# Moving one PSUM bank from the QKV projection to the attention scores in a fused attention and linear kernel

## The chip, the cores and the metric

The kernel runs on all 8 cores of one Trainium2 chip. Each core takes one of 8 batch entries and the cores exchange nothing. Time is device microseconds (us) of the slowest core, lower is better.

## What is computed

For each batch entry x of 2048 x 2048 (tokens x features): layer norm, a causal attention with 16 heads of width 128, layer norm and residual, then a linear layer with binarized weights, layer norm and residual. The attention has no exponentials: it takes the fourth power of the scores.

```python
def _L0_attn_ref(x, w_qkv, w_out, ln_scale, ln_bias):
    proj = x @ w_qkv
    q, k, v = jnp.split(proj, 3, axis=-1)          # 16 heads of 128 each
    ...
    q = layernorm(apply_rope(q, cos, sin), ln_scale, ln_bias)
    k = layernorm(apply_rope(k, cos, sin), ln_scale, ln_bias)
    a = jnp.einsum('bhnd,bhmd->bhnm', q, k) ** 4
    a = jnp.tril(a)
    out = jnp.einsum('bhnm,bhmd->bhnd', a / jnp.sum(a, -1, keepdims=True), v)
    return out.reshape(b, n, e) @ w_out
x = x + _layernorm(_L0_attn_ref(_layernorm(x), ...))
x = x + _layernorm(_layernorm(x) @ binarized(weight).T + bias)
```

## The kernel before

A helper records the operations of each engine in program order and derives semaphore waits from the tiles that each operation reads and writes. An engine works its own list strictly in order, so the order in which units are recorded is the order on each engine.

Three stages follow each other behind fences. The first normalizes x and runs the heads, the second projects with w_out, the third is the linear layer. Only the first uses the tiles of this change.

The first stage keeps the normalized, transposed x in SBUF (LNXT) and goes over heads h = 0 to 16. Step h does the QKV projection of head h and, interleaved with it, the attention of head h - 1.

- Projection: `u_m(m)` for m = 0 to 15 (blocks of 128 tokens). TensorE accumulates 16 matmuls (line 342) into one PSUM bank PQ, 384 columns wide (q, k and v). VectorE then reads it three times: two multiplies for the rotation (lines 348 and 352) and a copy of v into VPAD (line 357). Two additions with sums (line 363) follow on VectorE and two squarings with sums on ScalarE (line 372). PQ has two banks, used in turn. After the 16 blocks come `u_smalls` (mean and variance), 16 `u_norm` (line 407) and `u_final` (transposes by DMA, then scaling on ScalarE, lines 433 and 437).
- Attention: for each of four query blocks i and key blocks j up to 4i + 3, `u_s` makes one score matmul into a PSUM bank PS (line 457), and ScalarE squares it (line 464, reading PS) and squares it again (line 467). On the diagonal VectorE multiplies 128 columns by a triangle (line 471). `u_pv` does the value matmuls (line 482) of unit j - 4. At the end of a query block the last four are done and VectorE and ScalarE make the quotient (lines 492 to 508). PS has two banks by j % 2. The value sums have four banks, PV. With PQ and PS that is all eight PSUM banks.

The order: 34 projection units and 45 attention units are merged. With SHIFT = 3 the blocks m = 0 to 3 are issued with no attention unit between them; behind each later block come one or two (19 by the end of block 15), and the other 26 run beside `u_smalls` and the norms, where TensorE has no projection. At the end of a head's step VectorE has the signs and sums of one piece of the linear layer's weight (`swt_unit`, lines 566 to 579).

Of the kernel before, what the change touches and what calls it, by code (L numbers as in the profile page):

```python
# [8 lines left out]
F32 = mybir.dt.float32  # L9
# [172 lines left out]
def build_nc():  # L182
    nc = bass.Bass("TRN2", target_bir_lowering=False)
# [17 lines left out]
    P = Prog()  # L201
    with contextlib.ExitStack() as top:
# [48 lines left out]
        with contextlib.ExitStack() as sA:  # L251
            TA = sA.enter_context
# [16 lines left out]
            T1 = [TA(nc.sbuf_tensor(f"T1{i}", [128, 256], F32)) for i in range(2)]  # L269
# [11 lines left out]
            VPAD = [TA(nc.sbuf_tensor(f"VPAD{i}", [128, MC * 129], BF16))  # L281
                    for i in range(2)]
            S2B = [TA(nc.sbuf_tensor(f"S2B{i}", [128, 512], BF16)) for i in range(4)]
            S4B = [TA(nc.sbuf_tensor(f"S4B{i}", [128, 512], BF16)) for i in range(6)]
            PQ = [TA(nc.psum_tensor(f"PQ{i}", [128, 512], F32)) for i in range(2)]
            PS = [TA(nc.psum_tensor(f"PS{i}", [128, 512], F32)) for i in range(2)]
            PV = [TA(nc.psum_tensor(f"PV{i}", [128, 512], F32)) for i in range(4)]

            for i in range(2):
# [43 lines left out]
            def qkv_units(h):  # L333
                par = h % 2
                units = []
                wkeys = [f"wh{par}/{t_i}" for t_i in range(3)]

                def u_m(m):
                    b = m % 2
                    pqk = f"pq{b}"  # L340
                    for kc in range(KC):
                        P.op("t", lambda t, m=m, kc=kc, par=par, b=b: t.matmul(  # L342
                            PQ[b][:, 0:384],
                            LNXT[:, kc * N + m * 128: kc * N + m * 128 + 128],
                            WH[par][:, kc * 384:(kc + 1) * 384],
                            start=(kc == 0), stop=(kc == KC - 1)),
                            reads=[f"lnxT/{kc}/{m}"] + wkeys, writes=[pqk])
                    P.op("v", lambda v, b=b, m=m: v.tensor_tensor(  # L348
                        T1[b][:], PQ[b][:, 0:256],
                        AP(CT, m * 128, [[MC * 128, 128], [0, 2], [1, 128]]),  # L350
                        AOT.mult), reads=[pqk, "CT"], writes=[f"t1{b}"])
                    P.op("v", lambda v, b=b, m=m: v.tensor_tensor(  # L352
                        T2[b][:],
                        AP(PQ[b], 64, [[512, 128], [128, 2], [-64, 2], [1, 64]]),
                        AP(ST, m * 128, [[MC * 128, 128], [0, 2], [1, 128]]),
                        AOT.mult), reads=[pqk, "ST"], writes=[f"t2{b}"])
                    P.op("v", lambda v, b=b, m=m, par=par: v.tensor_copy(  # L357
                        VPAD[par][:, m * 129: m * 129 + 128], PQ[b][:, 256:384]),
                        reads=[pqk], writes=[f"vpad{par}/{m}"])
                    for t_i in range(2):  # L360
                        col = 2 * m + t_i
                        P.op("v", lambda v, b=b, m=m, t_i=t_i, col=col:
                             v.scalar_tensor_tensor(  # L363
                                 QR[:, m * 256 + t_i * 128:
                                    m * 256 + t_i * 128 + 128],
                                 T1[b][:, t_i * 128:(t_i + 1) * 128], cp(C_ZERO),
                                 T2[b][:, t_i * 128:(t_i + 1) * 128],
                                 AOT.add, AOT.add,
                                 accum_out=SUMS[:, col:col + 1]),
                             reads=[f"t1{b}", f"t2{b}", "CP0"],  # L370
                             writes=[f"qr/{m}/{t_i}", f"sums/{col}"])
                        P.op("s", lambda s, m=m, t_i=t_i, col=col: s.activation(  # L372
                            P4S[col % 4][:],
                            QR[:, m * 256 + t_i * 128: m * 256 + t_i * 128 + 128],
                            ACTF.Square, accum_out=SS[:, col:col + 1]),
                            reads=[f"qr/{m}/{t_i}"],
                            writes=[f"p4s{col % 4}", f"ssq/{col}"])
                for m in range(MC):
                    units.append(lambda m=m: u_m(m))

                def u_smalls():
                    sumkeys = [f"sums/{c_}" for c_ in range(32)]
                    sskeys = [f"ssq/{c_}" for c_ in range(32)]
                    P.op("v", lambda v: v.tensor_scalar(
                        MEANS[:], SUMS[:], cp(C_I128), None, AOT.mult,
                        AOT.bypass), reads=sumkeys + ["CP1"], writes=["means"])
                    P.op("v", lambda v: v.tensor_scalar(
                        SMA[:], SS[:], cp(C_I128), None, AOT.mult, AOT.bypass),
                        reads=sskeys, writes=["sma"])
                    P.op("v", lambda v: v.tensor_tensor(  # L390
                        SMB[:], MEANS[:], MEANS[:], AOT.mult),
                        reads=["means"], writes=["smb"])
                    P.op("v", lambda v: v.tensor_tensor(
                        SMA[:], SMA[:], SMB[:], AOT.subtract),
                        reads=["sma", "smb"], writes=["sma"])
                    P.op("s", lambda s: s.activation(
                        SMB[:], SMA[:], ACTF.Sqrt, bias=cp(C_EPS)),
                        reads=["sma"], writes=["smb"])
                    P.op("v", lambda v: v.reciprocal(RQ[:], SMB[:]),  # L399
                         reads=["smb"], writes=["rq"])  # L400
                units.append(u_smalls)

                def u_norm(m):
                    for t_i in range(2):
                        col = 2 * m + t_i
                        P.op("v", lambda v, m=m, t_i=t_i, col=col:
                             v.tensor_scalar(  # L407
                                 QN[:, t_i * N + m * 128:
                                    t_i * N + m * 128 + 128],
                                 QR[:, m * 256 + t_i * 128:  # L410
                                    m * 256 + t_i * 128 + 128],
                                 MEANS[:, col:col + 1], RQ[:, col:col + 1],
                                 AOT.subtract, AOT.mult),
                             reads=[f"qr/{m}/{t_i}", "means", "rq"],
                             writes=[f"qn/{m}/{t_i}"])
                for m in range(MC):
                    units.append(lambda m=m: u_norm(m))

                def u_final():
                    qnkeys = [f"qn/{m}/{t}" for m in range(MC)  # L420
                              for t in range(2)]
                    for t_i, dst, nm in ((0, QFM, "qfm"), (1, KFM, "kfm")):
                        P.dma("y", lambda y, t_i=t_i, dst=dst, par=par:
                              y.dma_start_transpose(
                                  AP(dst[par], 0,
                                     [[N, 128], [128, 16], [1, 128]]),
                                  QN[:, t_i * N:(t_i + 1) * N]),
                              reads=qnkeys,
                              writes=[f"{nm}{par}/{m}" for m in range(MC)],
                              slot=f"qnT{t_i}")  # L430
                    qk = [f"qfm{par}/{m}" for m in range(MC)]
                    kk = [f"kfm{par}/{m}" for m in range(MC)]
                    P.op("s", lambda s, par=par: s.activation(
                        QFM[par][:], QFM[par][:], ACTF.Identity, bias=BET[:],
                        scale=GAM[:]),
                        reads=qk + ["GAM", "BET"], writes=[f"qfmF{par}"] + qk)
                    P.op("s", lambda s, par=par: s.activation(
                        KFM[par][:], KFM[par][:], ACTF.Identity, bias=BET[:],
                        scale=GAM[:]),
                        reads=kk + ["GAM", "BET"], writes=[f"kfmF{par}"] + kk)  # L440
                units.append(u_final)
                return units

            def attn_units(hh):
# [4 lines left out]
                def u_s(i, j):  # L449
# [1 line left out]
                    s0 = 128 * max(0, r)  # L451
                    nj = 512 - s0
                    jb = j % 6
                    pb_ = j % 2
                    psk = f"ps{pb_}"
                    P.op("t", lambda t, i=i, j=j, s0=s0, nj=nj, pb_=pb_,
                         par=par: t.matmul(  # L457
# [458 lines left out]
```

How the kernel before makes its waits and increments, by code:

```python
    def emit_one(self, e, eng, sems, slot_sems):  # L135
        waited = {}
        drained = -1
        for i, op in enumerate(self.streams[e]):
            for sk, val in op.dma_waits:
                hs = slot_sems[sk]
                if waited.get(id(hs), -1) < val:
                    eng.wait_ge(hs, val)
                    waited[id(hs)] = val
            for dep, dval in op.deps:
                if dep.slot is not None:
                    hs = slot_sems[dep.slot]
                    val = dval
                else:
                    hs = sems[dep.eng]
                    val = dep.cum
                if waited.get(id(hs), -1) < val:
                    eng.wait_ge(hs, val)
                    waited[id(hs)] = val
            if op.drain_upto > drained:
                eng.drain()
                drained = i - 1
            if op.fn is None:
                if op.inc and e in sems:
                    eng.nop().then_inc(sems[e], 1)
                continue
            inst = op.fn(eng)
            if op.slot is not None:
                inst.then_inc(slot_sems[op.slot], 16)
            elif op.inc:
                inst.then_inc(sems[e], 1)
```

## Time and profile before

| | |
|---|---|
| median of 2 runs | 2498.98 us (2496.86 to 2501.1) |
| the profiled execution's own time | 2510.83 us |
| its span, slowest core (core 5) | 2509.3 us |
| spans of the 8 cores | 2462.0 to 2509.3 us |
| PE busy | 1629.7 us (65%), 8960 matmuls |
| ACT busy | 1200.3 us (48%) |
| DVE busy | 1014.7 us (40%) |

PE is TensorE's matmul side and PEld its weight loads, DVE is VectorE, ACT is ScalarE, POOL is GpSimd. Busy shares are means over the three stages. A timeline row gives an engine's work merged over like instructions; the last duration of a run of matmuls includes the pipeline's depth, so a block of 16 reads 2.76 us although blocks can follow each other every 2.60. PEclk is the granted TensorE clock, 1.00 for 2.4 GHz and 0.50 for 1.2 GHz. The brackets name the idle time before an instruction and what ended it.

### The profile page before, as it was taken

The page shows a single profiled execution, that of the slowest core. Times are in us where ns is not written, and L with a number is a line of the kernel's source. Part 1 is how long each engine was busy: PE and PEld are TensorE (multiplying, and loading weights), DVE is VectorE, ACT ScalarE, POOL GpSimd, SP SyncE. Part 2 cuts the span into 40 slices and gives each one's busy share as a digit, 9 for nine tenths or more (in the row PEclk, how much of TensorE's full clock was granted, in tenths as well). Part 3 has the DMA queues.
Part 4 walks back from the last instruction along what each step waited for, and adds up shares of the span by engine and source line. Part 5 has one row for each costly group of instructions (what it writes and reads, how often), then busy time and mean ns, then how long its engine had stood idle before and what let it go on. Part 6 is the DMA issues. An engine that isn't in the chain of part 4 may idle for free.

```text
span 2509.3 us, 32780 instructions; the slowest of 8 cores (2462.0 to 2509.3 us)
## 1 busy us (share of the span) xinstructions
PE 1629.7 (65%) x8960; PEld 860.8 (34%) x8960; DVE 1014.7 (40%) x3706; ACT 1200.3 (48%) x2865; POOL 170.5 (7%) x212
## 2 busy tenths in 40 slices
PE   0017797788778778877877895497555520298681
PEld 0004454454445444544544452243222210043230
DVE  3855554455555545554555554101212225002124
ACT  0002667766665776677567667512222225024334
POOL 1010000000000000000000000000000001100000
PEclk9998887798889779878977885598777765599895
DMA  8794065056235505532551433954455545834554
GB/s 105 197 168 51 1 85 80 8 82 85 46 40 85 84 14 73 85 54 32 85 85 23 63 60 60 184 148 103 117 151 117 117 118 159 291 77 128 157 138 172
DMA packets 428805, 246.50 MB, mean 98 GB/s; under 512 B 403776, under 2 KB 403776, under 8 KB 418384
## 3 DMA queue, kind: packets, MB, share of 16 engines
q0 software_dynamic: 159312, 177.26, 32.7%
q1 hardware_dynamic: 269312, 67.14, 16.8%
q8 instruction: 75, 1.23, 0.2%
q14 instruction: 106, 0.87, 0.1%
HBM read 160.47 MB, written 58.72 MB: 87 GB/s over the span
## 4 chain that ended last, share of the span: by engine, by line
PE 32%; ACT 22%; DMA 16%; issue 13%; DVE 11%; SPq 5%; ACTq 0%; DVEq 0%; POOL 0%; POOLq 0%
PE PQ L342 22%; ACT S2B L464 9%; DMA APJ<-APJT 5%; DMA YTM<-YTT 4%; PE PC L789 3%; DMA XB<-xb 3%; PE PB L661 3%; PE PS L457 2%; ACT S4B L467 2%; SPq L671 2%; PE PV L482 2%; DVE O L701 2%; ACT P4S L372 1%; SPq L800 1%; ACT SCB L709 1%
## 5 line engine op out<-in xcount | busy, mean ns | idle before, releaser
L342 PE MATMUL PQ<-WH,LNXT 128*128 128x384 bf16 x4096 | 729.1, 335 | 191.7 <-DMA WH<-wqkv 177.3
L342 PEld LDWEIGHTS PQ<-WH,LNXT 128*128 128x128 bf16 x4096 | 405.0, 100 | 472.9 <-issue 229.9
L457 PE MATMUL PS<-QFM,KFM 128*128 128x512 bf16 (+3 forms) x640 | 268.9, 436 | 218.0 <-ACT S2B L464 203.0
L467 ACT ACTIVATE S4B<-S2B 128x512 bf16<-128x512 bf16 (+3 forms) x640 | 361.9, 566 | 59.0 <-ACT S2B L464 0.4
L661 PE MATMUL PB<-ATK,LNXT 128*128 128x512 bf16 x1024 | 247.5, 408 | 186.3 <-ACT APJT L667 154.8
L789 PE MATMUL PC<-LX,LNXT 128*128 128x512 bf16 x1024 | 236.4, 395 | 178.3 <-DMA LX<-lnx2t_sc 142.4
L464 ACT ACTIVATE S2B<-PS 128x512 bf16<-128x512 f32 (+3 forms) x640 | 328.9, 514 | 0.8 <-PE PS L457 0.8
L482 PE MATMUL PV<-VPAD,S4B 128*128 128x129 bf16 x2176 | 285.1, 276 | 49.7 <-DVE S4B L471 44.9
L372 ACT ACTIVATE P4S<-QR 128x128 f32<-128x128 f32 x512 | 153.6, 300 | 309.6 <-DVE QR L363 309.2
L482 PEld LDWEIGHTS PV<-VPAD,S4B 128*128 128x128 bf16 x2176 | 208.7, 121 | 140.2 <-issue 117.3
L471 DVE TENSOR_TENSOR S4B<-S4B,TRI 128x128 bf16<-128x128 bf16 x256 | 57.5, 225 | 424.0 <-ACT S4B L467 402.8
L661 PEld LDWEIGHTS PB<-ATK,LNXT 128*128 128x128 bf16 x1024 | 105.3, 104 | 328.2 <-issue 224.1
L789 PEld LDWEIGHTS PC<-LX,LNXT 128*128 128x128 bf16 x1024 | 103.0, 101 | 311.7 <-issue 201.0
L457 PEld LDWEIGHTS PS<-QFM,KFM 128*128 128x128 bf16 x640 | 64.2, 100 | 339.5 <-issue 326.1
L348 DVE TENSOR_TENSOR T<-PQ,CT 128x256 f32<-128x256 f32 x256 | 107.8, 421 | 149.4 <-PE PQ L342 149.0
L363 DVE SCALAR_TENSOR_TENSOR QR<-T,CP 128x128 f32<-128x128 f32 x512 | 158.0, 345 | 1.8 <-DVE VPAD L357 1.5
L407 DVE TENSOR_SCALAR QN<-QR,MEANS,RQ 128x128 bf16<-128x128 f32 x512 | 140.3, 340 | 2.8 <-DVE RQ L399 2.7
L232 DVE TENSOR_SCALAR BS<-BS,CP 128x1 f32<-128x1 f32 x32 | 6.9, 214 | 324.2 <-ACT SCB L686 322.5
L686 ACT ACTIVATE SCB<-APJ 128x2048 bf16<-128x2048 bf16 x16 | 30.5, 1905 | 197.0 <-DMA APJ<-APJT 197.0
L232 DVE TENSOR_SCALAR CS<-CS,CP 128x1 f32<-128x1 f32 x16 | 3.4, 212 | 256.7 <-ACT SCC L815 256.7
L352 DVE TENSOR_TENSOR T<-PQ,ST 128x256 f32<-128x256 f32 x256 | 106.3, 415 | 0.0
L508 DVE TENSOR_SCALAR OUTH<-PV,RINV 128x128 bf16<-128x128 f32 x256 | 72.1, 344 | 68.0 <-ACT RINV L501 68.0
(86 smaller groups left out, 1153.6 us busy)
## 6 DMA issues: line engine op xcount, KB each, us to landing
XB<-xb POOLq DMA_DIRECT2D x32, 1024.0 KB, 9.5
WH<-wqkv POOLq DMA_DIRECT2D x48, 512.0 KB, 10.3
out_sc<-O POOLq DMA_DIRECT2D x16, 1024.0 KB, 4.2
O1R<-out_sc POOLq DMA_DIRECT2D x16, 1024.0 KB, 9.6
out<-OC POOLq DMA_DIRECT2D x16, 1024.0 KB, 5.6
XB<-fw POOLq DMA_DIRECT2D x16, 512.0 KB, 14.1
attnt_sc<-AFM POOLq DMA_DIRECT2D x16, 512.0 KB, 3.7
swt_sc<-XB POOLq DMA_DIRECT2D x16, 512.0 KB, 11.6
```

What stands on the lines that cost most here:

```text
L342: P.op("t", lambda t, m=m, kc=kc, par=par, b=b: t.matmul(PQ[b][:, 0:384], LNXT[:, kc * N + m * 128: kc * N + m * 128 + 128], WH[par][:, kc ...
L348: P.op("v", lambda v, b=b, m=m: v.tensor_tensor(T1[b][:], PQ[b][:, 0:256], AP(CT, m * 128, [[MC * 128, 128], [0, 2], [1, 128]]), AOT.mult) ...
L352: P.op("v", lambda v, b=b, m=m: v.tensor_tensor(T2[b][:], AP(PQ[b], 64, [[512, 128], [128, 2], [-64, 2], [1, 64]]), AP(ST, m * 128, [[MC * ...
L363: v.scalar_tensor_tensor(QR[:, m * 256 + t_i * 128: m * 256 + t_i * 128 + 128], T1[b][:, t_i * 128:(t_i + 1) * 128], cp(C_ZERO), T2[b][:, ...
L372: P.op("s", lambda s, m=m, t_i=t_i, col=col: s.activation(P4S[col % 4][:], QR[:, m * 256 + t_i * 128: m * 256 + t_i * 128 + 128], ACTF.Squ ...
L407: v.tensor_scalar(QN[:, t_i * N + m * 128: t_i * N + m * 128 + 128], QR[:, m * 256 + t_i * 128: m * 256 + t_i * 128 + 128], MEANS[:, col:c ...
L457: par=par: t.matmul(PS[pb_][:, 0:nj], KFM[par][:, j * 128:(j + 1) * 128], QFM[par][:, i * 512 + s0:(i + 1) * 512], start=True, stop=True),
L464: P.op("s", lambda s, j2=j2, pb_=pb_, nj=nj: s.activation(S2B[j2][:, 0:nj], PS[pb_][:, 0:nj], ACTF.Square), reads=[psk], writes=[f"s2{j2}"])
L467: P.op("s", lambda s, jb=jb, j2=j2, nj=nj: s.activation(S4B[jb][:, 0:nj], S2B[j2][:, 0:nj], ACTF.Square), reads=[f"s2{j2}"], writes=[f"s4{ ...
L482: par=par, i=i: t.matmul(PV[sub][:, 0:129], S4B[jb][:, 128 * sub - s0: 128 * sub - s0 + 128], VPAD[par][:, j * 129: j * 129 + 129], start= ...
L661: P.op("t", lambda t, s_=s_, kc=kc, pb=pb, tbb=tbb: t.matmul(PB[pb][:], LNXT[:, kc * N + s_ * 128: kc * N + s_ * 128 + 128], ATK[tbb][:, k ...
L789: P.op("t", lambda t, s_=s_, kc=kc, pb=pb, tbb=tbb: t.matmul(PC[pb][:], LNXT[:, kc * N + s_ * 128: kc * N + s_ * 128 + 128], LX[tbb][:, kc ...
```

## The change

The projection has one PSUM bank instead of two, and the scores have three instead of two, used by j % 3. The order of all operations, their number and their shapes stay as they are; T1, T2, VPAD and all SBUF tiles keep their buffers.

```diff
--- before.py
+++ after.py
@@ -282,8 +282,8 @@
                     for i in range(2)]
             S2B = [TA(nc.sbuf_tensor(f"S2B{i}", [128, 512], BF16)) for i in range(4)]
             S4B = [TA(nc.sbuf_tensor(f"S4B{i}", [128, 512], BF16)) for i in range(6)]
-            PQ = [TA(nc.psum_tensor(f"PQ{i}", [128, 512], F32)) for i in range(2)]
-            PS = [TA(nc.psum_tensor(f"PS{i}", [128, 512], F32)) for i in range(2)]
+            PQ = [TA(nc.psum_tensor(f"PQ{i}", [128, 512], F32)) for i in range(1)]
+            PS = [TA(nc.psum_tensor(f"PS{i}", [128, 512], F32)) for i in range(3)]
             PV = [TA(nc.psum_tensor(f"PV{i}", [128, 512], F32)) for i in range(4)]
 
             for i in range(2):
@@ -337,25 +337,25 @@
 
                 def u_m(m):
                     b = m % 2
-                    pqk = f"pq{b}"
+                    pqk = "pq0"
                     for kc in range(KC):
-                        P.op("t", lambda t, m=m, kc=kc, par=par, b=b: t.matmul(
-                            PQ[b][:, 0:384],
+                        P.op("t", lambda t, m=m, kc=kc, par=par: t.matmul(
+                            PQ[0][:, 0:384],
                             LNXT[:, kc * N + m * 128: kc * N + m * 128 + 128],
                             WH[par][:, kc * 384:(kc + 1) * 384],
                             start=(kc == 0), stop=(kc == KC - 1)),
                             reads=[f"lnxT/{kc}/{m}"] + wkeys, writes=[pqk])
                     P.op("v", lambda v, b=b, m=m: v.tensor_tensor(
-                        T1[b][:], PQ[b][:, 0:256],
+                        T1[b][:], PQ[0][:, 0:256],
                         AP(CT, m * 128, [[MC * 128, 128], [0, 2], [1, 128]]),
                         AOT.mult), reads=[pqk, "CT"], writes=[f"t1{b}"])
                     P.op("v", lambda v, b=b, m=m: v.tensor_tensor(
                         T2[b][:],
-                        AP(PQ[b], 64, [[512, 128], [128, 2], [-64, 2], [1, 64]]),
+                        AP(PQ[0], 64, [[512, 128], [128, 2], [-64, 2], [1, 64]]),
                         AP(ST, m * 128, [[MC * 128, 128], [0, 2], [1, 128]]),
                         AOT.mult), reads=[pqk, "ST"], writes=[f"t2{b}"])
-                    P.op("v", lambda v, b=b, m=m, par=par: v.tensor_copy(
-                        VPAD[par][:, m * 129: m * 129 + 128], PQ[b][:, 256:384]),
+                    P.op("v", lambda v, m=m, par=par: v.tensor_copy(
+                        VPAD[par][:, m * 129: m * 129 + 128], PQ[0][:, 256:384]),
                         reads=[pqk], writes=[f"vpad{par}/{m}"])
                     for t_i in range(2):
                         col = 2 * m + t_i
@@ -451,7 +451,7 @@
                     s0 = 128 * max(0, r)
                     nj = 512 - s0
                     jb = j % 6
-                    pb_ = j % 2
+                    pb_ = j % 3
                     psk = f"ps{pb_}"
                     P.op("t", lambda t, i=i, j=j, s0=s0, nj=nj, pb_=pb_,
                          par=par: t.matmul(
```

## Rows read from the trace of the kernel before

**Rows 1.** Waits, whole span: who waited for whom, us in total, times, longest.

```profile
PE PS L457 <- ACT S2B L464: 203.0, 362, 2.2
...
PE PQ L342 <- DVE VPAD L357: 13.3, 7, 10.0
```

**Rows 2.** Costliest groups: count | busy, mean ns | idle before, releaser.

```profile
L464 ACT ACTIVATE S2B<-PS 128x512 bf16<-128x512 f32 (+3 forms) x640 | 328.9, 514 | 0.8 <-PE PS L457 0.8
```

**Rows 3.** Timeline, one head, PE: start us, us, what [idle before <-releaser].

```profile
849.49 12.49 PE L342 MATMUL PQ<-WH,LNXT 128*128 128x384 bf16 x64
...
878.95 2.76 PE L342 MATMUL PQ<-WH,LNXT 128*128 128x384 bf16 x16
...
884.59 0.33 PE L457 MATMUL PS<-QFM,KFM 128*128 128x384 bf16 x1
...
885.32 2.76 PE L342 MATMUL PQ<-WH,LNXT 128*128 128x384 bf16 x16
...
936.49 1.76 PE L342 MATMUL PQ<-WH,LNXT 128*128 128x384 bf16 x5
```

**Rows 4.** Timeline, the same head, DVE.

```profile
855.39 0.17 DVE L579 TENSOR_TENSOR ALPHACC<-ALPHACC,ALPHA 128x16 f32<-128x16 f32 x1
855.50 0.42 DVE L348 TENSOR_TENSOR T<-PQ,CT 128x256 f32<-128x256 f32 x1
...
862.09 0.42 DVE L348 TENSOR_TENSOR T<-PQ,CT 128x256 f32<-128x256 f32 x1 [1.11 <-PE PQ L342]
...
865.60 0.42 DVE L348 TENSOR_TENSOR T<-PQ,CT 128x256 f32<-128x256 f32 x1
...
869.61 0.42 DVE L348 TENSOR_TENSOR T<-PQ,CT 128x256 f32<-128x256 f32 x1
...
881.82 0.42 DVE L348 TENSOR_TENSOR T<-PQ,CT 128x256 f32<-128x256 f32 x1 [1.65 <-PE PQ L342]
...
901.28 0.42 DVE L348 TENSOR_TENSOR T<-PQ,CT 128x256 f32<-128x256 f32 x1 [1.32 <-PE PQ L342]
```

**Rows 5.** Timeline, the same head, ACT, its second part.

```profile
923.50 0.58 ACT L464 ACTIVATE S2B<-PS 128x512 bf16<-128x512 f32 x1
...
924.71 0.58 ACT L464 ACTIVATE S2B<-PS 128x512 bf16<-128x512 f32 x1
```

**Rows 6.** Timeline, another head, all engines, a wait for the v copy.

```profile
768.71 0.42 DVE L348 TENSOR_TENSOR T<-PQ,CT 128x256 f32<-128x256 f32 x1 [0.28 <-issue]
...
769.38 0.28 DVE L357 CAST VPAD<-PQ 128x128 bf16<-128x128 f32 x1
...
769.81 0.49 PE L342 MATMUL PQ<-WH,LNXT 128*128 128x384 bf16 x2 [0.96 <-DVE VPAD L357]
```

**Rows 7.** Timeline, DVE, heads 0 (first two rows) and 1.

```profile
184.60 0.42 DVE L348 TENSOR_TENSOR T<-PQ,CT 128x256 f32<-128x256 f32 x1 [1.04 <-PE PQ L342]
...
221.00 0.42 DVE L348 TENSOR_TENSOR T<-PQ,CT 128x256 f32<-128x256 f32 x1 [1.11 <-PE PQ L342]
...
234.98 0.42 DVE L348 TENSOR_TENSOR T<-PQ,CT 128x256 f32<-128x256 f32 x1
...
240.39 0.42 DVE L348 TENSOR_TENSOR T<-PQ,CT 128x256 f32<-128x256 f32 x1 [2.51 <-PE PQ L342]
...
253.65 0.42 DVE L348 TENSOR_TENSOR T<-PQ,CT 128x256 f32<-128x256 f32 x1 [1.33 <-PE PQ L342]
...
290.62 0.42 DVE L348 TENSOR_TENSOR T<-PQ,CT 128x256 f32<-128x256 f32 x1 [1.32 <-PE PQ L342]
```

**Rows 8.** Stretches: us; busy us (x) of PE, PEld, DVE, ACT, POOL; PEclk; DMA; GB/s.

```profile
862.00:901.00 39.00, 36.45 (x243) 22.07 (x242) 21.91 (x108) 22.61 (x81) 4.51 (x5) 1.00 0.62 80
...
926.00:931.00 5.00, 2.45 (x21) 1.35 (x20) 0.00 (x0) 4.63 (x10) 0.00 (x0) 1.00 0.00 0
...
933.00:936.00 3.00, 2.31 (x19) 1.51 (x16) 1.84 (x10) 2.31 (x7) 0.00 (x0) 0.50 0.00 0
```

**Rows 9.** Timeline, PE, head 1, a block at the lower clock.

```profile
248.91 4.63 PE L342 MATMUL PQ<-WH,LNXT 128*128 128x384 bf16 x16
```

## Prediction

> **What bounds the kernel now.** I read four views, in this order: the waits, the costliest groups, the timeline of one head engine by engine, and the busy time and granted clock of short stretches. The waits come first because the change moves one PSUM bank from the projection (PQ) to the scores (PS), and they say how often either lack is felt. PE waited for a score bank, that is for ACT to square the scores, 362 times and 203.0 us in all; it waited for a projection bank, that is for DVE's copy of v, 7 times and 13.3 us [rows 1]. So at first sight the change gives a bank to the tile that lacks one. The second reading corrects that: ACT, which reads the score banks, waited for PE's scores 0.8 us in all [rows 2]. PE is ahead of ACT there, and a wait of PE that ends with a busy ACT is only the sign of who is slower.
>
> The timeline of one head shows why [rows 3, 4]. A head takes 87.0 us, from the projection that starts at 849.49 to the next at 936.49. In its first part, up to some 901, PE does 16 projection blocks (each 16 matmuls, some 2.6 us at the full clock) and about 19 attention units between them; PE is nearly always busy and sets the pace. In the second part, 901 to 936.5, there are no projections; ACT squares scores twice for every unit, at 1.21 us each, back to back, and sets the pace: the rows of ACT show one squaring every 1.21 us with no idle time [rows 5]. The two stages behind the loop of heads use other PSUM tiles and are not touched.
>
> **What is removed: the second projection bank.** Block m+1 may start only when DVE has read block m out, and the reader that comes last is the v copy (line 357), behind two multiplies (lines 348, 352). Three pieces of a cycle can be read:
> - from the start of a block on PE to the first multiply on DVE: 881.82 - 878.95 = 2.87 us [rows 3, 4];
> - from that multiply to the end of the copy: 769.38 + 0.28 - 768.71 = 0.95 us [rows 6];
> - from the end of the copy to PE's next matmul: the trace of before has this very wait. The copy ends at 769.38 + 0.28 = 769.66 and PE starts at 769.81, 0.15 us later [rows 6].
>
> The cycle is 2.87 + 0.95 + 0.15 = 3.97 us, of which PE computes projections for 2.6 us. Today blocks with nothing between them start 2.60 us apart: head 0 has 14 intervals between the multiplies of its second and sixteenth block, (221.00 - 184.60) / 14 = 2.60 [rows 7]. So a boundary without other work costs 3.97 - 2.60 = 1.37 us.
>
> With attention work between two blocks, that work hides in the wait, so the boundary costs less, but the spacing still can't fall under 3.97. The work in between is 0.22 us for one score matmul and 0.73 us for two units with value matmuls (884.59 to 885.32) [rows 3], under the 1.10 us of release (0.95 + 0.15). At the end of the first two query blocks it is ten value matmuls, the last behind a triangle multiply; but that multiply stands ahead of the v copy on DVE, so it too is done before the release. Other chains can make a boundary longer than 3.97: DVE's order puts the triangle multiply (line 471) of a diagonal unit ahead of the next block's multiply, and it waits for ACT, which waits for the sums of the block before. Their lengths are 865.60 - 862.09 = 3.51 us and 869.61 - 865.60 = 4.01 us [rows 4]. The second is 0.04 over the cycle and comes twice in a head; the first is under it. So in the new kernel nearly all boundaries are 3.97.
>
> A head from its first multiply to its last: before, 901.28 - 855.50 = 45.78 us [rows 4]; after, 15 x 3.97 + 2 x 0.04 = 59.63. That is +13.9 us. The start of the first multiply does not move: at 855.39 DVE has just finished its weight-sign work of the head before (855.39 + 0.17), which hangs on the end of attention, and PE's block 0 was done by then [rows 4]. What follows the last multiply does not shrink: the sums, ACT's second part of the head, the norms and the transposes all start from it, and ACT is full. There is no slack at the end of a head either: PE goes from the last value matmuls straight to the next projection at 936.49. So each of heads 2 to 15 pays 13.9 us in full.
>
> Heads 0 and 1 differ. Head 0 has no attention beside it: 15 boundaries x 1.37 = 20.6 us. In head 1 the start is covered: PE waits anyway for the first QFM/KFM, and its first multiplies come late because DVE is at the norms of head 0. From the first multiply at 234.98, block 1 starts at 236.08, its multiply is at 240.39 (a stretch at the lower clock), then two cycles give 248.33 and a third 252.30, against 253.65 today for block 4; from there 11 x 3.97 gives 295.97 for the last, against 290.62 [rows 7]. So +5.4 us.
>
> Sum: 20.6 + 5.4 + 14 x 13.9 = 221 us (rounded). Head 16 has no projection.
>
> **What is added: the third score bank.** PE can run one score matmul further ahead. In the second part of a head that buys nothing, since ACT has no gap there that PE causes (0.8 us in the whole span [rows 2]). In the first part PE's few waits for a score bank would vanish, but they lie between two blocks and so inside the new cycle of 3.97. The upper bound of the gain is all of PE's 203.0 us [rows 1]; I take 0, by the row nearest to the resource, which is ACT's. With j % 3 two scores in a row use bank 0 where the fourth unit of a head is followed by the fifth; a projection block and the end of the first query block lie between them, so I take nothing for it.
>
> **Clock.** The granted clock is 0.50 at the end of ACT's part of a head (933 to 936) and 1.00 in PE's part (862 to 901), that is 1.2 and 2.4 GHz [rows 8]. The new cycle has PE busy 2.6 of 3.97 us, 65%, where no attention work fills it. The trace has no long stretch like this. Nearest from below: 926 to 931 was 49% busy (2.45 of 5.00 us) at full clock and the clock had fallen by 933 (0.50); from above: 862 to 901 was 93% busy and kept it [rows 8]. A block that runs for the most part at the lower clock takes 4.63 us instead of 2.76 [rows 3, 9], 1.87 more. 65% is nearer to 49 than to 93, but most boundaries carry attention work and are at some 80%. Only the bare ones are in doubt: 15 in head 0 and 3 in each of 14 heads, 57. I take 0; the other end is 57 x 1.87 = 107 us. Block 0 of a head runs at the lower clock and ends at about 849.49 + 4.63 = 854.1, and block 1 has to wait to 855.50 + 1.10 = 856.6; in this gap of 2.5 us the clock may fall too, which is among the 57.
>
> The Trainium skill, "TensorE: Matmul & The Clock Gate", section on HAM oscillation, speaks against a large effect: it reports of a kernel whose matmuls ran long over K that adding PSUM double-buffering gave no further gain. By that the second projection bank would be worth about nothing and the sum would be near 0 instead of 221 us. The DVE rows above don't bear it out for blocks of 2.6 us with a read-out of 0.95 us behind them; no run here shows it.
>
> **Time.** The profiled execution took 2510.8 us (span 2509.3 and 1.5 around it). 2510.8 + 221 = 2732. The runs shown have a median of 2499.0, 11.8 lower; I keep that distance: 2720 us.
>
> **Rivals.**
> - A, forecast: the cycle of 3.97 us in every block, 2720. Chance 0.74.
> - B, the same and the clock falls in half of the bare blocks: + 53 us, 2773 (at most 2827). For it: 65% is a load that the trace doesn't show at full clock. Against it: the stretch from 862 to 901 has PE idle for 2.55 us in all, gaps between blocks among it, at 1.00 throughout [rows 8]. Chance 0.14.
> - C, only bare boundaries cost: attention work and waits that exist already cover the rest. In the head shown the fourth multiply would come after 855.50 + 3 x 3.97 = 867.41 instead of 862.09, 5.3 us: 14 x 5.3 + 20.6 = 95, so 2499 + 95 = 2594. Against it: work between blocks covers a release only if it exceeds 1.10 us, and it is 0.22 to 0.73. Chance 0.06.
> - D, no cost and no gain: DVE reads out so promptly that the single bank suffices, as 7 waits in 256 blocks might suggest; 2499. Against it: those 7 are waits with a whole spare bank. Chance 0.03. (It is also what the sentence of the Trainium skill, in "TensorE: Matmul & The Clock Gate", would give; the trace disagrees so far.)
> - E, faster: the third score bank gives back PE's 203.0 us and the release is covered: 2499 - 203 = 2296. The point from which it decides: what it gives must exceed what the release costs; at 221 us even the whole 203.0 doesn't. Its condition, ACT idle for lack of scores, is 0.8 us. Chance 0.03.
>
> The range of 8 in 10 holds A and most of B. Below A, the release without its 0.15 us latency takes 237 x 0.15 = 36 off (15 boundaries in 15 heads, 12 in head 1), 2684, and I leave some 25 for cover that I missed: 2660. Above, half of B's bound and a part more: 2800. It leaves out C, D, E and the top of B, 0.15 together. A measurement of this kernel can tell about 2% from no change; faster by over 2% is E, 0.03; within 2% is D, 0.03; slower is A, B and C, 0.94.
>
> **What would show it.** Right: PE's wait for the v copy of line 357 grows from 13.3 us to roughly 200 us or more over some 230 waits; the spacing of line 348's first multiplies in a head is 3.97 us; a head is 101 us long; PE's wait for score banks changes little or shrinks while ACT's second part keeps its 1.21 us. Wrong on the clock: matmuls of line 342 with a mean well above the 335 ns of now, and 0.50 in the first part. Wrong for C: spacings under 3.9 in blocks 4 to 15. Wrong for A as a whole: if ACT's second part gets shorter, or if DVE starts the multiplies otherwise than 2.87 us behind a block's start.

## The result and the profile after

| | before | after |
|---|---|---|
| median of all runs | 2515.4 us (10 runs) | 2760.9 us (11 runs) |
| ratio | | 1.100, 95% interval 1.095 to 1.105 |
| span of the profiled execution | 2509.3 us (core 5) | 2783.1 us (core 0) |
| head 0's first to head 15's last multiply of line 348, core 5 | 1329.3 us | 1574.0 us |
| PE busy | 1629.7 us | 1700.8 us |

The change costs 10%. Some executions fall in a slower state of the chip, in which the cores of one die show a lower granted clock; the ratios, and all times given for the experiments, are of executions outside it. The forecast was 2720 us with 2660 to 2800 as range; the measured median is 41 us above the value and inside the range. Of these 41 us, 16 are the kernel before, whose median over ten runs is that much above the two runs that the prediction had; the other 25 are the loss, 246 us instead of 221.

The waits of the changed kernel (core 0, the slowest; us in total, times, longest). PE's wait for the v copy, [rows 1], went from 13.3 us and 7 times to 250.9 us and 240 times. There are 240 boundaries between the 256 blocks inside the 16 heads. ScalarE also waits longer for the sums of VectorE (584.4 us, before 309.2); I read this as PE's delay passed on.

```profile
ACT P4S L372 <- DVE QR L363: 584.4, 238, 20.8
...
PE PQ L342 <- DVE VPAD L357: 250.9, 240, 11.2
...
PE PS L457 <- ACT S2B L464: 167.9, 312, 2.2
```

The costliest groups. The line of ScalarE's score squaring has the same 0.8 us of waiting as in [rows 2], with a third bank to read from. The matmuls of line 342 have a mean of 350 ns where they had 335 (340 to 342 on cores 3 to 7): a part of them ran at a lower clock, of which more below.

```profile
L342 PE MATMUL PQ<-WH,LNXT 128*128 128x384 bf16 x4096 | 784.6, 350 | 432.1 <-DVE VPAD L357 250.9
...
L464 ACT ACTIVATE S2B<-PS 128x512 bf16<-128x512 f32 (+3 forms) x640 | 328.5, 513 | 0.8 <-PE PS L457 0.8
```

The timeline of one head of core 0, PE first, then VectorE (start us, us). The blocks at 1016.58, 1020.55 and 1024.52 are 3.97 us apart, the second boundary with a score matmul in it and the first without.

```profile
1003.94 4.46 PE L342 MATMUL PQ<-WH,LNXT 128*128 128x384 bf16 x16
1011.05 4.33 PE L342 MATMUL PQ<-WH,LNXT 128*128 128x384 bf16 x16 [2.65 <-DVE VPAD L357]
1016.58 2.76 PE L342 MATMUL PQ<-WH,LNXT 128*128 128x384 bf16 x16 [1.21 <-DVE VPAD L357]
1020.55 2.76 PE L342 MATMUL PQ<-WH,LNXT 128*128 128x384 bf16 x16 [1.21 <-DVE VPAD L357]
1023.15 0.38 PE L457 MATMUL PS<-QFM,KFM 128*128 128x512 bf16 x1
1024.52 2.76 PE L342 MATMUL PQ<-WH,LNXT 128*128 128x384 bf16 x16 [0.99 <-DVE VPAD L357]
```

```profile
1009.84 0.17 DVE L579 TENSOR_TENSOR ALPHACC<-ALPHACC,ALPHA 128x16 f32<-128x16 f32 x1
1009.95 0.42 DVE L348 TENSOR_TENSOR T<-PQ,CT 128x256 f32<-128x256 f32 x1
...
1020.12 0.28 DVE L357 CAST VPAD<-PQ 128x128 bf16<-128x128 f32 x1
...
1023.42 0.42 DVE L348 TENSOR_TENSOR T<-PQ,CT 128x256 f32<-128x256 f32 x1 [2.47 <-PE PQ L342]
...
1024.09 0.28 DVE L357 CAST VPAD<-PQ 128x128 bf16<-128x128 f32 x1
...
1027.39 0.42 DVE L348 TENSOR_TENSOR T<-PQ,CT 128x256 f32<-128x256 f32 x1 [0.38 <-PE PQ L342]
```

From the block's start at 1020.55 to its first multiply at 1023.42 it is 2.87 us, from there to the end of the copy (1024.09 + 0.28) 0.95 us, and PE starts 0.15 us later. These are the three pieces of the prediction, each to 0.01 us. In head 8 of core 0 the multiplies lie 3.96 to 3.98 us apart from the second block on, but for two boundaries at 4.02.

ScalarE in its part of the head keeps 1.21 us for one unit, as in [rows 5]:

```profile
1088.52 0.58 ACT L464 ACTIVATE S2B<-PS 128x512 bf16<-128x512 f32 x1
...
1089.73 0.58 ACT L464 ACTIVATE S2B<-PS 128x512 bf16<-128x512 f32 x1
```

And over all heads, on the core that [rows 4] come from (core 5): the first multiply of head 0 and the last of head 15, two lines of before and two of after.

```profile
182.07 0.42 DVE L348 TENSOR_TENSOR T<-PQ,CT 128x256 f32<-128x256 f32 x1 [16.83 <-PE PQ L342]
...
1511.33 0.42 DVE L348 TENSOR_TENSOR T<-PQ,CT 128x256 f32<-128x256 f32 x1 [1.32 <-PE PQ L342]
```

```profile
193.65 0.42 DVE L348 TENSOR_TENSOR T<-PQ,CT 128x256 f32<-128x256 f32 x1 [20.11 <-PE PQ L342]
...
1767.64 0.42 DVE L348 TENSOR_TENSOR T<-PQ,CT 128x256 f32<-128x256 f32 x1 [2.47 <-PE PQ L342]
```

That is 1574.0 us, where before it was 1511.33 - 182.07 = 1329.3: 244.7 us more, as much as the whole loss (2760.9 - 2515.4 = 245.5). The two stages behind the heads use neither tile.

### The profile page after: what moved, and what is told of

Read it like the earlier page. It is cut to its first block, busy times and chain, and to the rows that moved or that the text cites. A ratio compares the mean times of both kernels' runs of the same rounds, so it can differ in the third digit from the quotient of the medians.

```text
span 2783.1 us, 32701 instructions; the slowest of 8 cores (2704.3 to 2783.1 us)
## 1 busy us (share of the span) xinstructions
PE 1700.8 (61%) x8960; PEld 858.6 (31%) x8960; DVE 1022.6 (37%) x3706; ACT 1202.4 (43%) x2865; POOL 169.8 (6%) x212
## 4 chain that ended last, share of the span: by engine, by line
PE 30%; ACT 19%; DVE 17%; DMA 14%; issue 14%; SPq 4%; DVEq 0%; ACTq 0%; POOL 0%; POOLq 0%
PE PQ L342 23%; ACT S2B L464 8%; DMA APJ<-APJT 4%; DVE T L348 4%; DMA YTM<-YTT 3%; PE PC L789 3%; DMA XB<-xb 3%; PE PB L661 3%; DVE VPAD L357 2%; SPq L671 2%; ACT S4B L467 1%; DVE O L701 1%; DMA LNXT<-swt_sc 1%; ACT SCB L709 1%; ACT SCB L690 1%
## 5 line engine op out<-in xcount | busy, mean ns | idle before, releaser
L342 PE MATMUL PQ<-WH,LNXT 128*128 128x384 bf16 x4096 | 784.6, 350 | 432.1 <-DVE VPAD L357 250.9
L372 ACT ACTIVATE P4S<-QR 128x128 f32<-128x128 f32 x512 | 153.8, 301 | 584.7 <-DVE QR L363 584.4
L457 PE MATMUL PS<-QFM,KFM 128*128 128x512 bf16 (+3 forms) x640 | 264.7, 437 | 183.5 <-ACT S2B L464 167.9
L482 PEld LDWEIGHTS PV<-VPAD,S4B 128*128 128x128 bf16 x2176 | 202.2, 118 | 146.2 <-issue 124.9
L524 POOL DMA_DIRECT2D attnt_sc<-AFM x16 | 9.0, 565 | 1563.7 <-DMA AFM<-OUTH 1563.7
```

The lines of the kernel that those rows point to most:

```text
L342: P.op("t", lambda t, m=m, kc=kc, par=par: t.matmul(PQ[0][:, 0:384], LNXT[:, kc * N + m * 128: kc * N + m * 128 + 128], WH[par][:, kc * 38 ...
L372: P.op("s", lambda s, m=m, t_i=t_i, col=col: s.activation(P4S[col % 4][:], QR[:, m * 256 + t_i * 128: m * 256 + t_i * 128 + 128], ACTF.Squ ...
L457: par=par: t.matmul(PS[pb_][:, 0:nj], KFM[par][:, j * 128:(j + 1) * 128], QFM[par][:, i * 512 + s0:(i + 1) * 512], start=True, stop=True),
L482: par=par, i=i: t.matmul(PV[sub][:, 0:129], S4B[jb][:, 128 * sub - s0: 128 * sub - s0 + 128], VPAD[par][:, j * 129: j * 129 + 129], start= ...
```

## The experiments

The first two take the change apart.

**The removal alone.** Two score banks instead of three:

```diff
-PS = [... f"PS{i}" ... for i in range(3)]
+PS = [... f"PS{i}" ... for i in range(2)]
-pb_ = j % 3
+pb_ = j % 2
```

> One projection bank, two score banks: the removal alone. Theory (the release of the single projection bank sets a cycle of 3.97 us and the third score bank is worth nothing): the time of the changed kernel, 2760 us within 15, ratio to the kernel before 1.10; the first multiplies of a head still 3.97 us apart, ACT's wait for scores still under 1 us. Rival 1 (the third score bank pays something back): over 2775. Rival 2 (part of the loss comes from the scores' new bank order, j % 3): under 2740.

Measured: 2748.2 us, ratio 1.096 (1.088 to 1.103), beside 2760.9 and 1.100 (1.095 to 1.105) of the changed kernel. The first multiplies are 3.97 us apart, and ScalarE waits 0.8 us for scores, both as expected. The waits (core 3):

```profile
PE PQ L342 <- DVE VPAD L357: 250.8, 240, 11.2
...
PE PS L457 <- ACT S2B L464: 209.0, 347, 2.2
```

The wait for the projection bank is within 4 us of the changed kernel's (254.6 us on the same core). The wait for score banks is 209.0 us here and 172.9 in the changed kernel on the same core; on core 0 it is 185.7 and 167.9, on core 5 186.0 and 183.1. So the third bank takes 3 to 36 us off a wait of PE, by the core, and nothing that can be measured off the time: the two kernels differ by less than their intervals, which leave room for some 20 us. Neither rival holds.

**The addition alone.** The bank for it is taken from the value sums:

```diff
-PS = [... range(2)]     # j % 2
-PV = [... range(4)]
+PS = [... range(3)]     # j % 3
+PV = [... range(3)]
-PV[sub][:, 0:129], ... start=(j == 0), stop=(j == 4 * i + sub)
+PV[min(sub, 2)][:, 0:129], ... start=(j == 0 and sub < 3), stop=(j == 4 * i + sub and sub != 2)
```

> Two projection banks and three score banks: the addition alone. The eighth bank comes from the value sums: the fourth quarter of a query block is added into the third quarter's bank, so the output for these two quarters is wrong; all instructions and their number stay. Theory: the time of the kernel before, ratio 1.00 within 0.005, since ACT waited for scores 0.8 us in all; PE's wait for score banks may fall without any effect. Rival (score banks are what the heads lack): up to 203 us less, ratio down to 0.92.

Measured: ratio 0.9997 (0.996 to 1.004). The waits (core 3):

```profile
PE PS L457 <- ACT S2B L464: 170.6, 313, 2.2
...
PE PQ L342 <- DVE VPAD L357: 12.6, 6, 10.0
```

PE's wait for score banks fell by 24 to 43 us (on core 3 from 194.3 to 170.6, on core 0 from 209.6 to 166.9), and the kernel took the same time. So a wait of the engine that is ahead is no measure of a bank's worth.

**The size of the release.** If the read-out sets the cycle, a longer read-out must lengthen it block by block. The v copy (line 357) is recorded twice, once with the single bank and once in the kernel before:

```diff
 P.op("v", ... VPAD[par][...] <- PQ[0][:, 256:384] ...)
+P.op("v", ... VPAD[par][...] <- PQ[0][:, 256:384] ...)
```

> The changed kernel with the v copy done twice: the read-out of the single bank is longer by one copy, 0.20 us from start to start. Theory: the cycle is 4.17 instead of 3.97 us, and 237 boundaries x 0.20 = 47 us more than the changed kernel, about 2808 us. Rival (the wait of PE is covered or set by something else, ACT's chain): less than 15 us more.

> The kernel before with the v copy done twice. Theory: with a spare bank the read-out lies beside PE's next block; only the two or three boundaries of a head that hang on the chain DVE, ACT, triangle multiply can get 0.20 us longer: 0 to 12 us more than the kernel before, ratio 1.000 to 1.005. Rival (DVE's time is the cost with two banks too): 47 us more, 1.019.

Measured: with one bank 2863.5 and 2867.3 us, some 104 us more than the changed kernel instead of 47. With two banks ratio 1.024 (1.020 to 1.029), 61 us more instead of at most 12, and more than the rival's 47 too. VectorE with one bank:

```profile
1045.71 0.42 DVE L348 TENSOR_TENSOR T<-PQ,CT 128x256 f32<-128x256 f32 x1 [4.16 <-PE PQ L342]
...
1046.38 0.29 DVE L357 CAST VPAD<-PQ 128x128 bf16<-128x128 f32 x1
1046.77 0.30 DVE L360 CAST VPAD<-PQ 128x128 bf16<-128x128 f32 x1
...
1050.08 0.42 DVE L348 TENSOR_TENSOR T<-PQ,CT 128x256 f32<-128x256 f32 x1 [2.48 <-PE PQ L342]
```

The second copy starts 0.39 us behind the first, and the additions of line 366 follow 0.20 us behind a copy: the second copy writes the same columns of VPAD and the helper makes it wait for the first (read from the kernel; no run has two copies without that wait). So the read-out grew by 0.40 us, not 0.20, and the multiplies are 1050.08 - 1045.71 = 4.37 us apart, 0.40 over 3.97. 240 x 0.40 = 96 us of the 104. My expectation had the right rule and the wrong size of the edit. For the kernel before it was wrong in kind: I had counted two or three boundaries on VectorE's chain. The time from first to last multiply grew from 45.7 to 49.1 us in a typical head: nine boundaries got longer, most by 0.40 us, among them all those between 3.0 and 4.0 us, and two got shorter. So with two banks VectorE's read-out is on the path in about half the boundaries of a head; with one bank it is in all of them. That led to the last experiments.

**Block 0 and block 1.** In the changed kernel the multiplies of blocks 0 and 1 are 5.5 us apart in most heads, 1.5 more than the cycle. The weight-sign work (lines 566 to 579) was moved off VectorE's list at that place:

```diff
-    swt_unit(h - 1)          # at the end of step h
+    if h >= 1 and iq == 24:  # behind the eighth norm unit of step h
+        swt_unit(h - 1)
```

> The changed kernel with VectorE's weight-sign work taken from between the end of a head and the read-out of the next head's block 0, and put behind the eighth norm unit of the next step. Theory (block 1 starts late because of that work, TensorE idles for 2.6 us and block 1 runs at the lower clock): the read-out of block 0 starts when its matmuls end, some 1.0 us earlier, and block 1 is at 3.97 behind it instead of 5.5: 14 heads x 2.5 = 35 us less than the changed kernel, about 2725. Rival (block 1 is slow because every head starts at the lower clock, whatever the gap): the spacing of blocks 0 and 1 stays near 5.5 and the time falls by 15 us at most.

> The kernel before with the same move of the weight-sign work. Theory: with two banks it delayed PE by 0.2 to 1.0 us in about half the heads; 0 to 10 us less than the kernel before, ratio 0.995 to 1.000. Rival (the work is on the path in every head, 4 us each): 50 us less.

Measured: with one bank 2710.2 us, ratio 1.079 (1.074 to 1.083), 51 us less than the changed kernel, where 35 were expected. With two banks ratio 0.998 (0.994 to 1.002), no difference. The first two multiplies of a head with one bank, and block 1 on PE:

```profile
875.19 0.42 DVE L348 TENSOR_TENSOR T<-PQ,CT 128x256 f32<-128x256 f32 x1 [3.52 <-PE PQ L342]
...
879.16 0.42 DVE L348 TENSOR_TENSOR T<-PQ,CT 128x256 f32<-128x256 f32 x1 [2.47 <-PE PQ L342]
```

```profile
876.29 2.76 PE L342 MATMUL PQ<-WH,LNXT 128*128 128x384 bf16 x16 [1.21 <-DVE VPAD L357]
```

They are 3.97 us apart, like nearly all others. PE is idle for 1.21 us before block 1, not 2.65, and block 1 takes 2.76 us at a granted clock of 1.00, so the rival (every head starts at the lower clock, whatever the gap) is out. A head is 99.4 us long instead of 102.5 (means over heads 7 to 15): 14 x 3.1 = 43 of the 51 us. The rest is not attributed. The kernel before never noticed this work because block 1 had its own bank.

**Another merge.** Since the first part of a head is bound by PE and the second by ScalarE, more attention units were put behind each block:

```diff
-want = int(round((iq + 1 - SHIFT) * len(ua) / max(1, len(uq) - SHIFT)))
+nb = min(iq + 1, MC) - SHIFT
+nt = max(0, iq + 1 - MC)
+full = 2.5 * (MC - SHIFT)
+want = int(round(2.5 * nb + (len(ua) - full) * nt / (len(uq) - MC)))
```

> The kernel before (two projection and two score banks) with another merge: 2.5 attention units behind each block from the fourth on (32 of 45) instead of 1.45. Theory (the first part of a head is bound by TensorE and the second by ScalarE): the second part loses 13 units x 1.21 = 16 us and the first gains at most 13 x 0.6 = 8 us of TensorE's work; 8 us less in each of 15 heads, 120 us, ratio about 0.95. Rival (the in-order queues of the three engines wait for each other, so the first part grows by ScalarE's full 1.21 us a unit): ratio 1.00.

> The changed kernel with the merge of 2.5 attention units behind each block. Theory: the cycle of 3.97 us has some 0.7 us in which TensorE is idle even beside attention work, so most of the moved units are free: the second part loses 16 us, the first gains 0 to 6 us; 150 to 230 us less than the changed kernel, 2530 to 2610. If the third score bank is of use anywhere, it is here, where one block is followed by three units. Rival (the chain DVE, ACT, triangle multiply sets the boundaries once more units lie in them): less than 60 us saved.

Measured: on the kernel before ratio 1.097 (1.090 to 1.105), on the changed one 1.116 (1.108 to 1.123). Both expectations were wrong, the first by some 350 us, the second by at least 188; the first rival (no change) was wrong as well, and the second (less than 60 us saved) held only in that nothing was saved. PE in one of the gaps of the first (kernel before with this merge, core 5):

```profile
1017.16 0.27 PE L457 MATMUL PS<-QFM,KFM 128*128 128x256 bf16 x1
1018.24 0.22 PE L457 MATMUL PS<-QFM,KFM 128*128 128x128 bf16 x1 [0.81 <-ACT S2B L464]
1018.37 0.39 PE L482 MATMUL PV<-VPAD,S4B 128*128 128x129 bf16 x4
1019.18 0.33 PE L482 MATMUL PV<-VPAD,S4B 128*128 128x129 bf16 x3 [0.43 <-DVE S4B L471]
1022.21 0.38 PE L482 MATMUL PV<-VPAD,S4B 128*128 128x129 bf16 x2 [2.69 <-DVE S4B L471]
1022.77 0.27 PE L482 MATMUL PV<-VPAD,S4B 128*128 128x129 bf16 x1 [0.19 <-DVE DEN L492]
1022.83 5.33 PE L342 MATMUL PQ<-WH,LNXT 128*128 128x384 bf16 x16
```

Here the units up to the end of a query block stand in one gap. PE may not start the next block, which needs nothing of them, until it has made the last value matmuls in its list, and these wait for ScalarE's squarings and the triangle multiply: 2.69 us at 1022.21. The block behind it then takes 5.33 instead of 2.76 us, at the lower clock (PEclk 0.50 from 1023 to 1028). From 1017.16 to 1022.83 it is 5.7 us for some 2 us of work. ScalarE gets to these squarings late because its list has the sums of the block (line 372) in front, which wait for VectorE:

```profile
1020.26 0.31 ACT L372 ACTIVATE P4S<-QR 128x128 f32<-128x128 f32 x1 [1.55 <-DVE QR L363]
```

**The sums of a block, later.** In the last group ScalarE's squarings with sums of block m are recorded at the start of block m + 1, behind the attention units of block m; with the merge of the kernel before, and with 2.0 and 1.7 units behind each block:

```diff
+def sq(m):                     # the two activations of line 372
+    ...
 def u_m(m):
+    if m:
+        sq(m - 1)
...
 def u_smalls():
+    sq(MC - 1)
```

> The kernel before, but ScalarE's squarings with sums of block m (line 372) are recorded at the start of block m + 1, behind the attention units of block m. Theory (in the kernel before the boundaries of 3.5 and 4.0 us come from the chain: sums on VectorE, squarings and score squarings on ScalarE, triangle multiply, next read-out): the chain loses its first link, the long boundaries shrink towards TensorE's 3.1 us, and PE's 2.6 us of idle time in the first part vanish: 20 to 35 us less than the kernel before, ratio 0.986 to 0.992. Rival (the long boundaries are PE's own work): no change.

> The kernel before with the late squarings and 2.0 attention units behind each block from the fourth on (26 of 45 instead of 19). Theory (the merge of 2.5 units was slow because in-order ScalarE held the score squarings behind the sums of the block): 7 units leave the second part, 8.5 us, and add some 4 us of TensorE's work to the first: 4.5 us in each of 15 heads more than the late squarings alone give, ratio about 0.96. Rival (it was slow because several units and a query block's end stand in one gap, so TensorE waits for ScalarE's squarings before it may do the next block): ratio 1.00 or above.

> The same with 1.7 units behind each block (22 of 45). Theory: between the late squarings alone and the merge of 2.0. Rival (units and a query block's end in one gap): the time depends on where the ends fall, not on the number of units, and may be above the one of 2.0.

Measured: the late sums alone ratio 0.978 (0.973 to 0.984), more than the 20 to 35 us expected; with 2.0 units 0.959 (0.951 to 0.968), 2400.9 us, as expected; with 1.7 units 0.982 (0.976 to 0.987), not between the two. ScalarE's wait for the sums in the kernel before, and the waits of the late sums alone (there lines are shifted by the edit: 341 is the sums, 471 the score squaring):

```profile
ACT P4S L372 <- DVE QR L363: 309.2, 210, 20.0
```

```profile
ACT P4S L341 <- DVE QR L375: 86.4, 62, 11.8
ACT S2B L471 <- PE PS L464: 81.3, 117, 1.5
```

ScalarE waited 309 us for the sums before and 86.4 us now. The time from first to last multiply in a head fell from 45.7 to 42.4 us; 15 x 3.3 = 50 us of some 55. It now waits 81.3 us for scores, where it waited 0.8 before: the long boundaries were no work of PE's but this chain. The version with 2.0 units beats both kernels of the study: a head takes 79.0 us instead of 87.0 (mean from head 8 to 15). That 1.7 units are slower than 2.0 fits the rival: it has two boundaries of 4.70 us in a head, the one with 2.0 has one. (Against the late sums alone, 0.982 and 0.978, its intervals overlap: it gains nothing, and that it loses is not shown.) By the merge's rule each of the three boundaries holds the last diagonal unit of a query block followed by that block's end; where an end comes first in its gap, the boundary is 3.6 to 3.9 us. That this order, and not the number of units, decides I read from these three boundaries; no run keeps the number and moves the ends. Nor was 2.5 run with the late sums, or 2.0 without them, so what part of the loss above came from the sums is open.

**A score bank fewer.**

```diff
-PS = [... range(2)]     # j % 2
+PS = [... range(1)]     # j % 1
```

> The kernel before with a single score bank: one bank fewer on the side where the changed kernel has one more. Theory (a bank more than the pair is worth nothing, but the second one covers TensorE's score matmul and the handing over beside ScalarE's second squaring of 0.63 us): the score squaring of line 464 is the only reader, and while ScalarE does line 467, 0.63 us, TensorE can refill the bank in 0.2 to 0.6 us; so little is lost in the second part, but in the first part the second of two units in a gap waits for ScalarE: 0 to 60 us more than the kernel before. Rival (the banks of the scores count like those of the projection): 200 us more.

Measured: ratio 1.083 (1.073 to 1.092), some 208 us more (two executions). The rival's size was right and mine was wrong. ScalarE's pace in its own part, and PE beside it:

```profile
1132.92 0.60 ACT L464 ACTIVATE S2B<-PS 128x512 bf16<-128x512 f32 x1
1133.61 0.63 ACT L467 ACTIVATE S4B<-S2B 128x512 bf16<-128x512 bf16 x1
1134.34 0.60 ACT L464 ACTIVATE S2B<-PS 128x512 bf16<-128x512 f32 x1
```

```profile
1133.66 0.58 PE L457 MATMUL PS<-QFM,KFM 128*128 128x512 bf16 x1 [0.41 <-ACT S2B L464]
...
1135.08 0.59 PE L457 MATMUL PS<-QFM,KFM 128*128 128x512 bf16 x1 [0.41 <-ACT S2B L464]
```

ScalarE takes 1.42 us for a unit instead of 1.21. It is the same sum as for the projection: the squaring that reads the bank 0.60, hand-over 0.14, the score matmul 0.58 (at the lower clock), hand-over 0.10, together 1.42; ScalarE's second squaring lies beside it and is over at 1134.24, just when the score matmul is. At the full clock nothing is lost: of the units of 512 columns that follow each other directly on this core, 31 of 32 at a granted clock of 1.00 took 1.20 to 1.21 us, and all 243 at 0.50 took 1.40 to 1.43. With two banks they took 1.21 at either clock. In PE's part it is worse: three boundaries of a head, those with two score matmuls in them, became 7.2 to 7.4 us in head 8 where they were 3.1 to 4.0. PE stands at the second score matmul until ScalarE has read the first, ScalarE is behind the sums of the block, and the projection block behind the wait runs partly at the lower clock (4.44 instead of 2.76 us):

```profile
981.50 0.27 PE L457 MATMUL PS<-QFM,KFM 128*128 128x256 bf16 x1 [3.02 <-ACT S2B L464]
981.63 4.44 PE L342 MATMUL PQ<-WH,LNXT 128*128 128x384 bf16 x16
```

From first to last multiply a head is some 10.5 us longer (56 against 45.7), behind that some 4. So in this kernel the second score bank is worth nearly what the second projection bank is, and the third nothing. A third projection bank was not tried; PE waited for one 7 times.

## Why the prediction was right, and where it was off

- *The cycle of 3.97 us.* Right in all three pieces (2.87, 0.95, 0.15), and shown by the removal alone and by the longer read-out, which lengthened every cycle by the 0.40 us it added.
- *Attention work between blocks hides in the wait, no boundary is shorter than 3.97, two are 4.01.* Right: 3.96 to 3.98 and twice 4.02. Rival C had boundaries under 3.9 in blocks 4 to 15; there is none.
- *The third score bank is worth 0.* Right, by both halves of the change measured alone. The reading that decided it was the 0.8 us of ScalarE in [rows 2] against the 203.0 us of PE in [rows 1].
- *Head 0: 20.6 us.* Measured 59.5 - 38.9 = 20.6.
- *Heads 2 to 15: 13.9 us each.* Measured 61.2 - 45.7 = 15.5 from first to last multiply. The missing 1.6 is the boundary of blocks 0 and 1. The step that failed is the clock: the prediction named the gap of 2.5 us before block 1, put it among the 57 doubtful boundaries and took 0 for all of them. Of these the 15 in head 0 and the other two in each head kept the clock, with a matmul block of 2.6 us in each 3.97, and block 1 lost it in most heads. The prediction's own sign of being wrong on the clock, a longer mean of line 342 and 0.50 in the first part of a head, came true in this one place. The windows of core 0 (us; PE, PEld, DVE, ACT, POOL busy; PEclk; DMA; GB/s) show it, with a stretch with 75% busy at full clock in the third line:

```profile
1009.00:1011.00 2.00, 0.00 (x0) 0.00 (x0) 1.90 (x6) 1.65 (x2) 0.00 (x0) 0.96 1.14 210
1011.00:1013.00 2.00, 1.95 (x7) 0.95 (x8) 0.44 (x4) 2.00 (x5) 0.00 (x0) 0.50 1.93 187
...
1020.00:1030.00 10.00, 7.52 (x45) 4.24 (x46) 4.15 (x21) 3.71 (x16) 0.83 (x1) 1.00 1.17 93
...
390.00:400.00 10.00, 7.98 (x46) 4.33 (x45) 3.81 (x18) 3.44 (x14) 0.00 (x0) 0.81 1.15 132
```

  PE had nothing to do from 1008.4 to 1011.05 (mean grant 0.96), and the grant was 0.50 as block 1 began; it took 4.33 instead of 2.76 us. 14 x 1.55 = 22 us, which together with 221 makes 243 of the 244.7 measured on core 5. That the weight-sign work makes this gap is shown by moving it, and with the gap the fall of the clock went too. The length of the gap alone does not decide, though: block 1 kept the full clock behind gaps of 1.8 us and of 3.2 us (heads 8 and 2 of core 3) and lost it behind 2.1 to 3.2 us in the others. What else decides is open.
- *Head 1: 5.4 us.* Too low: from its first multiply to that of head 2 it is 8.5 us more on core 5 and 11.8 on core 3. On core 5 the missing 3.1 are three boundaries: 0.4 at block 1; 1.0 between blocks 6 and 7, where VectorE is late with the quotient of a query block (4.97 us, in the kernel before too, where the prediction took 3.97); and 1.7 at block 8, which took 4.44 us at the lower clock. On cores 0 to 2 of the profiled execution the Q and K transposes of head 0 were also late, so block 4 waited (12.1 us between two multiplies on core 0). The pieces of this head I took from one core and one DMA timing. It is a small term.
- *How much of the nearness is luck.* Little: the loss was forecast as 221 and is 245, and both misses of size, 22 us of clock and 3 in head 1, have the same sign. The value 2720 rests besides on a median of two runs.
- *Rival B* (clock falls in half of the bare blocks, 53 us) had the right cause but was too wide: one bare block in a head, none of head 0. The Trainium skill's sentence on PSUM double-buffering ("TensorE: Matmul & The Clock Gate", HAM oscillation), which would have given rival D, does not carry over to these blocks: the spare bank is worth 10% here.

## What to carry to other kernels

A wait for a buffer counts only if the engine on the other side of the buffer also runs dry: PE's 203.0 us was worth nothing beside ScalarE's 0.8. For a single buffer add up the cycle (fill, first read, last read, hand-over); if it exceeds what the producer does for a block, the producer's other work hides in the wait as far as it fits (here 0.22 to 0.73 us in 1.10) and every block costs the cycle. In in-order queues, move work that waits long behind work that doesn't: the sums of a block behind the score squarings gave 2.2% by themselves and 4.1% with a fuller merge (2.0 units a block), while a still fuller one (2.5) without them cost 9.7%.

## What the hardware showed that I had not expected

The granted clock has a third value in these traces. On core 0, heads 2 to 4, and on core 1 at the same time, it was 0.81 from about 325 to 710 us, but for the stretches at 0.50; the fourth of the windows above is from there. The blocks then read 3.31 us instead of 2.76 and their cycle is 4.52:

```profile
396.44 3.31 PE L342 MATMUL PQ<-WH,LNXT 128*128 128x384 bf16 x16 [1.14 <-DVE VPAD L357]
...
400.96 3.31 PE L342 MATMUL PQ<-WH,LNXT 128*128 128x384 bf16 x16 [0.27 <-DVE VPAD L357]
```

Three heads of core 0 were 7.9 to 8.6 us longer, some 24 us, which is most of what this core had over core 5. Cores 2 and 3 of the same die, in blocks of the same stretch (400 to 410), were at 1.00, and so were cores 4 to 7. Cores 2 and 3 had 0.81 at another time, from about 2420 to 2700 us, when cores 0 and 1 did not: in this execution it came to two neighbouring cores together. The Trainium skill ("TensorE: Matmul & The Clock Gate", the section "Seeing it yourself") describes a limiter that takes a whole die to 13/16 of the clock when three of its cores run dense matmuls; the value agrees with 0.81, the whole die does not, and what set it off is open.
